# A tower of patch embedding, 16-head attention and a quantised layer: two pieces of the embedding weights loaded ahead of the second patch tile

## The chip, the core and the metric

The kernel runs on one core of a Trainium2 chip. The core has a matrix engine (TensorE, PE in the profile, with PEld for its weight loads), three engines for elementwise work (VectorE or DVE, ScalarE or ACT, GpSimd or POOL) and a sync engine (SP), which here issues all the transfers between the chip's main memory (HBM) and the on-chip memory. Each engine works through its own list of instructions in order; engines wait for one another by semaphores. The metric is the device time of one execution in microseconds (us).

## What is computed

```python
# tok: x (64, 125, 64) -> 448 rows of 1024 (64 batches x 7 patches)
x = x[:, :n_patch * TIN, :].reshape(bsz, n_patch, TIN * F)
x = layer_norm(x, g1, b1, 1e-6)
x = jnp.einsum('bpd,dh->bph', x, W) + b          # 1024 -> 512
h = layer_norm(x, g2, b2, 1e-6)
# attention: 16 heads of 128, causal, inside each batch of 7 rows
h = h + attn(layernorm(h, 1e-5))
# a linear layer on values rounded to fp8 with one scale for all
h = h + ffn(layernorm(h, 1e-5))
```

All of it is in fp32; products in attention and in the last layer are made of three fp32r products of high and low parts.

## The kernel before

The 448 rows are cut into four tiles of 112 rows (`TILES`, `TR`). The input width of 1024 is cut into eight chunks of 128 (`KIN`). For each tile t the embedding has these steps:

- `patch_moments(t)` on DVE (line 777 for the statistics, 779 for their aggregate) waits for the tile's patches; `rsqrt` turns the variance into a reciprocal root. For the tiles named in `ROOTS` ScalarE takes a square root first (`take_root`, line 569) and DVE mends it in three short steps (`rsqrt_from_root`, lines 795 to 805); for the others DVE works out the root alone in eight steps (lines 821 to 829). Line 837 makes the shift `nmr`.
- `normalise(t)` on ACT (line 574) applies scale and shift.
- `patch_transposes(t)` on PE (line 309) turns the eight chunks, `patch_evacuate(t)` on ACT (line 583) brings them back as `xt`, scaled by g1 and shifted by b1.
- `embed(t, half)` on PE (line 320) multiplies four chunks by `tokw_raw`, the weights of 1024 x 512, which come in four pieces of two chunks (`TOKW_PIECES`). After the second half a short product adds the bias (line 325). For tile 0 it waits for `tok_b_lo_ok`.
- `stream_norms` on DVE then normalises the embedded tile from `acc[t]`; `normalise_stream` (ACT, line 592), `stream_transposes` (PE, line 336), `stream_evacuate` (ACT) and `stream_lo` (DVE, line 770) give `ht_hi` and `ht_lo`, from which the attention's products of line 280 to 282 read. Three tiles must be there before the first of them.

The order is written out by hand in each engine's list. Three places of it matter here. SP issues its transfers in the order of lines 238 to 260, all in one queue, with no wait before the one of `ffn_b_cleared`. PE's list is the loop behind `patch_transposes(0)`: half of a tile's product, the next tile's transposes, the other half. And the bias is split into high and low part on two engines: ACT makes the high part at line 614 (shown as L563, the helper), behind `normalise(1)`; DVE makes the low part in `bias_lo` (shown as L770), which is placed inside the root of tile 2, behind its sixth step:

```python
need(rsqrt([(2, LN_EPS)], patch_moments(2), between=lambda i: bias_lo() if i == 5 else None))
```

So `bias_lo` comes behind `patch_moments(2)`, which waits for the patches of tile 2. Behind it DVE waits for `rows_landed` (g2 and b2, the last two transfers of this stage) before tile 3.

Of the kernel before, what the change touches and what calls it, by code (L numbers as in the profile page):

```python
# [21 lines left out]
TILES = 4  # L22
TR = ROWS // TILES
KIN = IN_DIM // 128
# [11 lines left out]
LN_EPS, NORM_EPS = 1e-6, 1e-5  # L36


ROOTS = {0: LN_EPS, 2 * TILES + 1: NORM_EPS, TILES + 2: LN_EPS, 2 * TILES + 2: NORM_EPS,
         TILES + 3: LN_EPS, 2 * TILES + 3: NORM_EPS}  # L40
FP8_MAX, SCALE_EPS = 448.0, 1e-7
SHIFT_20 = 2.0 ** 20
# [8 lines left out]
def audio_tower(nc, patches, tok_w, heads_w, ffn_w, tok_g1, tok_b1, tok_b, tok_g2, tok_b2,  # L51
# [4 lines left out]
    with ExitStack() as ctx:  # L56
        def sb(name, shape, dt=F32):
            return ctx.enter_context(nc.sbuf_tensor(name, shape, dt))

        def sem(name):  # L60
            return ctx.enter_context(nc.semaphore(name))
# [14 lines left out]
        x_in = sb("x_in", [TR, TILES, IN_DIM])  # L76
# [48 lines left out]
        nmr = sb("nmr", [TR, NCOL])  # L125
        eps_4 = sb("eps_4", [TR, len(ROOTS)])
        root = sb("root", [TR, len(ROOTS)])
        last_root = sb("last_root", [TR, TILES])
# [20 lines left out]
        x_landed = [sem(f"x_landed{t}") for t in range(TILES)]  # L149
# [72 lines left out]
        def loop_heads(eng, step):  # L222

            with eng.Fori(0, (HEADS - 2) // 2) as i:
                step(i * 2 + 1, i, 1)
                step(i * 2 + 2, i + 1, 0)


        @block.sync
        def _(sp):  # L230
            def load(dst, src, landed):
                sp.dma_start(dst, src).then_inc(landed, 16)  # L232

            def load_tokw(i):
                a, b = TOKW_PIECES[i]
                load(tokw_raw[:, a:b, :], tok_w[:, a:b, :], tokw_landed[i])

            for c, landed in ((slice(0, 512), x_landed[0]), (slice(512, IN_DIM), x0_rest_landed)):
                load(x_in[:, 0, c], patches[0][:, c], landed)
            load(ident_sb[:], ident, ident_landed)  # L240
            load(g1_col[:], tok_g1, cols_landed)
            load(b1_col[:], tok_b1, cols_landed)
            load(x_in[:, 1, :], patches[1], x_landed[1])
            load_tokw(0)
            load_tokw(1)
            load_tokw(2)
            load(x_in[:, 2, :], patches[2], x_landed[2])
            load_tokw(3)
            load(tok_b_raw[:], tok_b, tok_b_landed)
            load(x_in[:, 3, :], patches[3], x_landed[3])  # L250
            load(g2_row[:], tok_g2.to_broadcast([TR, D]), rows_landed)
            load(b2_row[:], tok_b2.to_broadcast([TR, D]), rows_landed)
            load(mask_sb[:], mask, late_landed)
            load(ffn_scale_col[:], ffn_scale.to_broadcast([128, 1]), late_landed)
            sp.wait_ge(ffn_b_cleared, 1)
            for row in (0, B_LO):
                load(ffn_b_raw[row:row + 1, :], ffn_bias, late_landed)
            for s in range(2):
                sp.dma_start(raw[:, s, :], heads_w[s]).then_inc(raw_landed[s], 16)
            sp.dma_start(ffnw_raw[:], ffn_w).then_inc(ffnw_landed, 16)  # L260

            def load_head(h, _, s):


                sp.wait_ge(outw_hi_ok, h)
                sp.wait_ge(outw_lo_ok, h)
                sp.dma_start(raw[:, 1 - s, :], heads_w[h + 1]).then_inc(raw_landed[1 - s], 16)

            loop_heads(sp, load_head)
            for i, (t, c) in enumerate(RESULTS):  # L270
                sp.wait_ge(y_ok, i + 1)
                sp.dma_start(out[t][:, c], h_sb[:, t, c]).then_inc(out_stored, 16)
            sp.wait_ge(out_stored, 16 * len(RESULTS))
# [3 lines left out]
        def _(pe):  # L277
# [19 lines left out]
            def patch_transposes(t):  # L297
                if t == 0:
                    pe.wait_ge(ident_landed, 16)
                    pe.wait_ge(x0_half_normed, 1)  # L300
                else:
                    pe.wait_ge(x_normed, t + 1)
                if t >= 2:
                    pe.wait_ge(xt_ok, KIN * (t - 1))
                for k in range(KIN):
                    if t == 0 and k == KIN // 2:
                        pe.wait_ge(x_normed, 1)
                    b = 2 * (t % 2) + k // 4
                    mm = nc.tensor.transpose(bank[b][:, k % 4 * TR:(k % 4 + 1) * TR],
                                             x_in[:, t, k * 128:(k + 1) * 128], ident_sb[0:TR, 0:TR])  # L310
                    if k % 4 == 3:
                        mm.then_inc(xt_ps, 1)

            def embed(t, half):
                for k in range(half * KIN // 2, (half + 1) * KIN // 2):
                    for i, (first_chunk, _) in enumerate(TOKW_PIECES):
                        if t == 0 and k == first_chunk:
                            pe.wait_ge(tokw_landed[i], 16)
                    pe.wait_ge(xt_ok, KIN * t + k + 1)
                    nc.tensor.matmul(acc[t][0:TR, :], xt[:, t % 2, k * TR:(k + 1) * TR], tokw_raw[:, k, :],  # L320
                                     start=(k == 0), stop=False, skip_group_check=True)
                if half == 1:
                    if t == 0:
                        pe.wait_ge(tok_b_lo_ok, 1)
                    nc.tensor.matmul(acc[t][0:TR, :], ones_r[:], tok_b_split[:], start=False, stop=True,
                                     skip_group_check=True).then_inc(tok_ps, 1)


            def stream_transposes(t):
                pe.wait_ge(hn_ok, t + 1)  # L330
                if t <= 1:
                    pe.wait_ge(xt_ok, KIN * (TILES - 1))
                if t == 2:
                    pe.wait_ge(xt_ok, KIN * TILES)
                for k in range(KD):
                    last = nc.tensor.transpose(ht_bank[t][:, k * TR:(k + 1) * TR],
                                               hn_sb[:, t, k * 128:(k + 1) * 128], ident_sb[0:TR, 0:TR])
                last.then_inc(ht_ps, 1)
# [14 lines left out]
            patch_transposes(0)  # L353
            for t in range(TILES):
                embed(t, 0)
                if t + 1 < TILES:
                    patch_transposes(t + 1)
                else:
                    stream_transposes(1)
                embed(t, 1)  # L360
                if t == TILES - 2:
                    stream_transposes(0)
# [198 lines left out]
        def _(act):  # L561
# [3 lines left out]
            def take_root(c):  # L565
                i = list(ROOTS).index(c)
                act.wait_ge(variance_ok, i + 1)
                act.wait_ge(eps_ok, len(ROOTS))
                nc.scalar.activation(root[:, i:i + 1], moments[:, c, 1:2], ACT.Sqrt, bias=eps_4[:, i:i + 1],
                                     scale=4.0).then_inc(root_ok, 1)  # L570

            def normalise(t, c=slice(0, IN_DIM)):
                act.wait_ge(x_scaled, t + 1)
                nc.scalar.activation(x_in[:, t, c], x_in[:, t, c], ACT.Identity, bias=nmr[:, t:t + 1],
                                     scale=rstd[:, t:t + 1]).then_inc(x_normed, 1)

            def patch_evacuate(t):
                for half in range(2):
                    act.wait_ge(xt_ps, 2 * t + half + 1)
                    if t >= 2 and half == 0:  # L580
                        act.wait_ge(tok_ps, t - 1)
                    for k in range(half * KIN // 2, (half + 1) * KIN // 2):
                        nc.scalar.activation(xt[:, t % 2, k * TR:(k + 1) * TR],  # L583
                                             bank[2 * (t % 2) + half][:, k % 4 * TR:(k % 4 + 1) * TR],
                                             ACT.Identity, bias=b1_col[:, k:k + 1],
                                             scale=g1_col[:, k:k + 1]).then_inc(xt_ok, 1)
# [22 lines left out]
            normalise(0, slice(IN_DIM // 2, IN_DIM))  # L609
            act.wait_ge(cols_landed, 32)  # L610
            patch_evacuate(0)
            normalise(1)
            act.wait_ge(tok_b_landed, 16)
            hi_part(tok_b_split[:], tok_b_raw[:]).then_inc(tok_b_hi_ok, 1)
# [138 lines left out]
        def _(dve):  # L753
# [18 lines left out]
            def moments_of(c, parts, rest_landed=None):  # L772
# [6 lines left out]
                aggregate = nc.vector.bn_aggr(moments[:, c, :], stats[:, c, 0:len(parts), :])  # L779
                if c not in ROOTS:  # L780
                    return mark(aggregate)
                aggregate.then_inc(variance_ok, 1)

            def need_moments(c, step):
                if c in ROOTS:
                    dve.wait_ge(variance_ok, list(ROOTS).index(c) + 1)
# [340 lines left out]
```

## Time and profile before

| | |
|---|---|
| median of 3 runs | 275.11 us (274.51 to 275.82) |
| the profiled execution | 274.97 us, span 273.2 us |
| PE busy | 263.6 us of the span |
| DVE busy, ACT busy | 156.8 us, 129.9 us |
| read from HBM | 22.56 MB |

In the profile L12 is line 12 of the kernel; times within the span are in us from its start. The last 1.8 us of the execution's own time lie outside the span. The attention heads fill the span from about 57 to 246 us with PE busy throughout; the stage that the change touches is the first 57 us. A row of a timeline gives start, duration, engine, line, operation, output and input, the count of instructions, and in brackets how long the engine stood idle before it and what released it. A matmul in fp32 stands in the profile as two instructions, so four chunks of line 320 are a row of x8.

### The profile page before, as it was taken

How to read it: one execution, taken by the hardware profiler on the slowest of the kernel's cores; microseconds unless marked ns; L12 is line 12 of the kernel's file. 1: busy time of each engine (PE TensorE's matmuls, PEld its weight loads, DVE VectorE, ACT ScalarE, POOL GpSimd, SP SyncE). 2: the span in 40 equal slices, each digit the busy share in tenths (PEclk: the TensorE clock that was granted, in tenths of full speed). 3: DMA queues.
4: the chain of work that ended last, by engine and by line, in shares of the span. 5: the costliest groups of instructions: out<-in, count | busy, mean ns of one | idle time of the engine just before them, and what ended most of it. 6: DMA issues, size and time to landing. Idle time of an engine off the chain costs nothing.

```text
span 273.2 us, 3833 instructions
## 1 busy us (share of the span) xinstructions
PE 263.6 (97%) x1444; PEld 220.4 (81%) x1444; DVE 156.8 (57%) x322; ACT 129.9 (48%) x221; POOL 0.2 (0%) x4
## 2 busy tenths in 40 slices
PE   7799998999999999999999999999999999999895
PEld 7434446999999999999999999999999999985363
DVE  6479969655555446263555455362645453579782
ACT  2663952454435444544535344435444354365460
POOL 0000000000000000000000000000000000000000
PEclk9999999999999999999999999999999999999799
DMA  6998000134214040403123040404132100000004
GB/s 191 309 289 366 2 0 1 29 127 154 82 74 151 2 154 0 154 6 148 52 102 116 37 154 0 154 0 154 17 137 86 67 0 0 0 4 0 0 0 134
DMA packets 5319, 23.57 MB, mean 86 GB/s; under 512 B 1005, under 2 KB 1469, under 8 KB 3136
## 3 DMA queue, kind: packets, MB, share of 16 engines
q1 hardware_dynamic: 5312, 23.48, 25.3%
q8 instruction: 4, 0.07, 0.1%
q14 instruction: 3, 0.02, 0.0%
HBM read 22.56 MB, written 0.92 MB: 86 GB/s over the span
## 4 chain that ended last, share of the span: by engine, by line
PE 75%; DVE 9%; ACT 5%; DMA 4%; SPq 3%; issue 2%; DVEq 0%; ACTq 0%
PE bank L280 15%; PE bank L281 15%; PE bank L282 15%; PE acc L422 8%; PE bank L406 5%; PE bank L398 5%; PE acc L426 4%; DMA b_row<-tok_b 4%; SPq L232 3%; PE bank L412 2%; PE bank L391 2%; PE acc L541 2%; ACT xt L583 2%; DVE stats L777 1%; DVE ffnw_lo L770 1%
## 5 line engine op out<-in xcount | busy, mean ns | idle before, releaser
L280 PE MATMUL bank<-ht_hi,qkvw_hi 128*128 128x448 f32 (+2 forms) x204 | 74.7, 366 | 0.1
L281 PE MATMUL bank<-ht_lo,qkvw_hi 128*128 128x448 f32 (+2 forms) x204 | 73.3, 359 | 0.0
L282 PE MATMUL bank<-ht_hi,qkvw_lo 128*128 128x448 f32 (+2 forms) x204 | 73.2, 359 | 0.0
L770 DVE TENSOR_TENSOR qkvw_lo<-raw,qkvw_hi 128x1536 fp32r<-128x1536 f32 x16 | 28.1, 1758 | 30.8 <-ACT qkvw_hi L563 30.8
L280 PEld LDWEIGHTS bank<-ht_hi,qkvw_hi 128*128 128x128 f32 x204 | 38.4, 188 | 3.3 <-issue 0.3
L282 PEld LDWEIGHTS bank<-ht_hi,qkvw_lo 128*128 128x128 f32 x204 | 38.3, 188 | 3.3
L281 PEld LDWEIGHTS bank<-ht_lo,qkvw_hi 128*128 128x128 f32 x204 | 38.4, 188 | 3.0
L770 DVE TENSOR_TENSOR z_lo<-bank,z_hi 128x448 fp32r<-128x448 f32 x15 | 9.4, 624 | 43.2 <-ACT z_hi L563 43.2
L320 PE MATMUL acc<-tokw_raw,xt 128*112 128x512 f32 x64 | 29.3, 598 | 1.5 <-DMA tokw_raw<-tok_w 1.5
L563 ACT CAST qkvw_hi<-raw 128x1536 fp32r<-128x1536 f32 x16 | 23.6, 1482 | 0.0
L320 PEld LDWEIGHTS acc<-tokw_raw,xt 128*112 128x112 f32 x64 | 10.6, 177 | 14.7 <-issue 9.6
L659 ACT COPY v_t<-bank 128x448 f32<-128x448 f32 x16 | 8.5, 532 | 28.4 <-PE bank L282 28.4
L422 PE MATMUL acc<-z_hi,outw_hi 128*128 128x448 f32 x56 | 21.7, 388 | 0.0
L651 ACT COPY q_t<-bank 128x448 f32<-128x448 f32 x16 | 8.5, 531 | 26.3 <-PE bank L282 26.3
L422 PE MATMUL acc<-z_hi,outw_lo 128*128 128x448 f32 x56 | 20.6, 368 | 0.0
L642 ACT ACTIVATE prob<-prob 112x448 f32<-112x448 f32 x16 | 9.3, 578 | 18.6 <-DVE prob L946 18.6
L398 PEld LDWEIGHTS bank<-prob_t,v_nat 112*128 112x128 f32 x128 | 16.7, 191 | 0.7
L398 PE MATMUL bank<-prob_t,v_nat 112*128 112x112 f32 x128 | 16.7, 273 | 0.0
L950 DVE TENSOR_REDUCE ssum<-prob 112x4 f32<-112x448 f32 x16 | 9.9, 619 | 9.9 <-ACT prob L642 9.9
L406 PE MATMUL bank<-k_t,q_t 128*112 128x112 f32 x128 | 15.2, 262 | 0.0
L663 ACT COPY v_nat<-bank 112x512 f32<-112x512 f32 x16 | 9.4, 587 | 10.4 <-PE bank L412 10.4
L406 PEld LDWEIGHTS bank<-k_t,q_t 128*112 128x112 f32 x128 | 13.9, 178 | 0.1
(128 smaller groups left out, 350.4 us busy)
## 6 DMA issues: line engine op xcount, KB each, us to landing
raw<-heads_w SPq DMA_DIRECT2D x16, 1024.0 KB, 4.8
tokw_raw<-tok_w SPq DMA_DIRECT2D x4, 512.0 KB, 7.1
x_in<-patches SPq DMA_DIRECT2D x3, 448.0 KB, 9.1
ffnw_raw<-ffn_w SPq DMA_DIRECT2D x1, 1024.0 KB, 16.8
out<-h_sb SPq DMA_DIRECT2D x3, 224.0 KB, 2.3
x_in<-patches SPq DMA_DIRECT2D x2, 224.0 KB, 2.9
g_row<-tok_g SPq DMA_DIRECT2D x1, 224.0 KB, 10.6
b_row<-tok_b SPq DMA_DIRECT2D x1, 224.0 KB, 11.1
```

The lines of the kernel that those rows point to most:

```text
L280: nc.tensor.matmul(ps, hi, whi, start=first, stop=False, skip_group_check=True)
L281: nc.tensor.matmul(ps, hi, wlo, start=False, stop=False, skip_group_check=True)
L282: return nc.tensor.matmul(ps, lo, whi, start=False, stop=last, skip_group_check=True)
L320: nc.tensor.matmul(acc[t][0:TR, :], xt[:, t % 2, k * TR:(k + 1) * TR], tokw_raw[:, k, :], start=(k == 0), stop=False, skip_group_check=True)
L398: last = nc.tensor.matmul(bank[b][:, t * TR:(t + 1) * TR], v_nat[:, t, :], prob_t[:, t, :], start=True, stop=True)
L406: last = nc.tensor.matmul(bank[1][0:TR, c], q_t[:, c], k_t[:, c], start=True, stop=True)
L422: nc.tensor.matmul(acc[c][:, 0:ROWS], w[:, c * 128:(c + 1) * 128], all_rows(z_hi), start=False, stop=False, skip_group_check=True)
L426: last = nc.tensor.matmul(acc[c][:, 0:ROWS], outw_hi[s][:, c * 128:(c + 1) * 128], all_rows(z_lo), start=False, stop=False, skip_group_che ...
L563: return nc.scalar.copy(dst, src)
L663: nc.scalar.copy(v_nat[:].rearrange("p t e -> p (t e)"), bank[3][0:TR, :]).then_inc(vn_ok, 1)
L770: return nc.vector.tensor_tensor(dst, src, hi.bitcast(F32), ALU.subtract)
L950: nc.vector.tensor_reduce(ssum[:], prob[:], AX.X, ALU.add).then_inc(softmax_step, 1)
```

## The change

The transfers of the first two weight pieces go ahead of tile 1's patches, and tile 2's patches go behind all four weight pieces and the bias. Tile 1 joins `ROOTS`, so ScalarE takes its square root ahead of `normalise(1)`. On PE tile 0's product is no longer cut in the middle: tile 1's transposes stand behind its seventh chunk, and the loop goes on to tile 1 with `continue`. Nothing else is moved; `bias_lo` keeps its place. Adding an entry to `ROOTS` also adds one short memset on DVE. In the later lines the numbers grow by 2 to 6.

```diff
-ROOTS = {0: LN_EPS, 2 * TILES + 1: NORM_EPS, TILES + 2: LN_EPS, 2 * TILES + 2: NORM_EPS,
+ROOTS = {0: LN_EPS, 1: LN_EPS, 2 * TILES + 1: NORM_EPS, TILES + 2: LN_EPS, 2 * TILES + 2: NORM_EPS,
...
-            load(x_in[:, 1, :], patches[1], x_landed[1])
             load_tokw(0)
             load_tokw(1)
+            load(x_in[:, 1, :], patches[1], x_landed[1])
             load_tokw(2)
-            load(x_in[:, 2, :], patches[2], x_landed[2])
             load_tokw(3)
             load(tok_b_raw[:], tok_b, tok_b_landed)
+            load(x_in[:, 2, :], patches[2], x_landed[2])
             load(x_in[:, 3, :], patches[3], x_landed[3])
...
-            def embed(t, half):
+            def embed(t, half, within=None):
...
+                    if k == KIN - 2 and within is not None:
+                        within()
...
                 embed(t, 0)
+                if t == 0:
+                    embed(t, 1, within=lambda: patch_transposes(1))
+                    continue
                 if t + 1 < TILES:
                     patch_transposes(t + 1)
...
             patch_evacuate(0)
+            take_root(1)
             normalise(1)
```

The first place is SP's queue at the start of the program. Patches are `x_in`, weight pieces `tokw_raw` (x2 are two of them). Before:

```order
L232 DMA b_col<-tok_b 128x8
L232 DMA x_in<-patches 112x1024
L232 DMA tokw_raw<-tok_w 128x1024 x3
L232 DMA x_in<-patches 112x1024
L232 DMA tokw_raw<-tok_w 128x1024
L232 DMA tok_b_raw<-tok_b 33x512
L232 DMA x_in<-patches 112x1024
L232 DMA g_row<-tok_g 112x512
```

And now:

```order
L232 DMA b_col<-tok_b 128x8
L232 DMA tokw_raw<-tok_w 128x1024 x2
L232 DMA x_in<-patches 112x1024
L232 DMA tokw_raw<-tok_w 128x1024 x2
L232 DMA tok_b_raw<-tok_b 33x512
L232 DMA x_in<-patches 112x1024 x2
L232 DMA g_row<-tok_g 112x512
```

Tile 2's patches moved past the last weight piece and the bias; what is issued up to and with the bias before is the same set of transfers that is now issued up to and with tile 2's patches.

The second place is PE from the first chunk of tile 0 to the first chunks of tile 1. Before:

```order
L320 MATMUL acc<-tokw_raw,xt 112x512 [waits xt_ok,tokw_landed0]
L320 MATMUL acc<-tokw_raw,xt 112x512 [waits xt_ok]
L320 MATMUL acc<-tokw_raw,xt 112x512 [waits xt_ok,tokw_landed1]
L320 MATMUL acc<-tokw_raw,xt 112x512 [waits xt_ok]
L309 MATMUL bank<-ident_sb,x_in 128x112 [waits x_normed]
L309 MATMUL bank<-ident_sb,x_in 128x112 x7
L320 MATMUL acc<-tokw_raw,xt 112x512 [waits xt_ok,tokw_landed2]
L320 MATMUL acc<-tokw_raw,xt 112x512 [waits xt_ok]
L320 MATMUL acc<-tokw_raw,xt 112x512 [waits xt_ok,tokw_landed3]
L320 MATMUL acc<-tokw_raw,xt 112x512 [waits xt_ok]
L325 MATMUL acc<-tok_b_split,ones_r 112x512 [waits tok_b_lo_ok]
L320 MATMUL acc<-tokw_raw,xt 112x512 [waits xt_ok] x4
```

And now:

```order
L320 MATMUL acc<-tokw_raw,xt 112x512 [waits xt_ok,tokw_landed2]
L320 MATMUL acc<-tokw_raw,xt 112x512 [waits xt_ok]
L320 MATMUL acc<-tokw_raw,xt 112x512 [waits xt_ok,tokw_landed3]
L309 MATMUL bank<-ident_sb,x_in 128x112 [waits x_normed]
L309 MATMUL bank<-ident_sb,x_in 128x112 x7
L320 MATMUL acc<-tokw_raw,xt 112x512 [waits xt_ok]
L327 MATMUL acc<-tok_b_split,ones_r 112x512 [waits tok_b_lo_ok]
L320 MATMUL acc<-tokw_raw,xt 112x512 [waits xt_ok] x4
```

The transposes of tile 1 (line 309) moved from behind the fourth chunk to behind the seventh; the bias product with its wait still stands ahead of all of tile 1's product.

The third place is DVE, from the end of tile 1's root to the low part of the bias. Before:

```order
L829 SCALAR_TENSOR_TENSOR rstd<-newton,rstd 112x1 [waits dve_step]
L837 SCALAR_TENSOR_TENSOR nmr<-moments,rstd 112x1 [waits dve_step]
L777 BN_STATS stats<-x_in 112x6 [waits x_landed2]
L777 BN_STATS stats<-x_in 112x6
L779 BN_AGGR moments<-stats 112x2 [waits dve_step]
L821 TENSOR_SCALAR vscaled<-moments 112x1 [waits dve_step]
L824 TENSOR_SCALAR rstd<-vscaled 112x1 [waits dve_step]
L827 TENSOR_SCALAR newton<-rstd,vscaled 112x1 [waits dve_step]
L829 SCALAR_TENSOR_TENSOR rstd<-newton,rstd 112x1 [waits dve_step]
L827 TENSOR_SCALAR newton<-rstd,vscaled 112x1 [waits dve_step]
L829 SCALAR_TENSOR_TENSOR rstd<-newton,rstd 112x1 [waits dve_step]
L770 TENSOR_TENSOR tok_b_split<-tok_b_raw,tok_b_split 1x512 [waits tok_b_hi_ok]
```

And now:

```order
L811 SCALAR_TENSOR_TENSOR rstd<-newton,rstd 112x1 [waits dve_step]
L843 SCALAR_TENSOR_TENSOR nmr<-moments,rstd 112x1 [waits dve_step]
L783 BN_STATS stats<-x_in 112x6 [waits x_landed2]
L783 BN_STATS stats<-x_in 112x6
L785 BN_AGGR moments<-stats 112x2 [waits dve_step]
L827 TENSOR_SCALAR vscaled<-moments 112x1 [waits dve_step]
L830 TENSOR_SCALAR rstd<-vscaled 112x1 [waits dve_step]
L833 TENSOR_SCALAR newton<-rstd,vscaled 112x1 [waits dve_step]
L835 SCALAR_TENSOR_TENSOR rstd<-newton,rstd 112x1 [waits dve_step]
L833 TENSOR_SCALAR newton<-rstd,vscaled 112x1 [waits dve_step]
L835 SCALAR_TENSOR_TENSOR rstd<-newton,rstd 112x1 [waits dve_step]
L776 TENSOR_TENSOR tok_b_split<-tok_b_raw,tok_b_split 1x512 [waits tok_b_hi_ok]
```

Tile 1's root now ends with line 811, behind ACT's square root. From the wait for tile 2's patches (`x_landed2`) on, DVE's list is as it was: the low part of the bias (L770, now L776) stands nine instructions behind that wait.

## Rows read from the trace of the kernel before

**Rows 1.** The chain in order of time, 0 to 45 us: start, us, what.

```profile
8.34 11.10 DMA b_row<-tok_b
```

**Rows 2.** Timeline of PE, 8.9 to 45.6 us.

```profile
9.17 3.69 PE L320 MATMUL acc<-tokw_raw,xt 128*112 128x512 f32 x8 [1.23 <-DMA tokw_raw<-tok_w]
12.70 0.93 PE L309 MATMUL bank<-ident_sb,x_in 112*128 112x112 f32 x8
13.47 1.88 PE L320 MATMUL acc<-tokw_raw,xt 128*112 128x512 f32 x4
15.60 1.97 PE L320 MATMUL acc<-tokw_raw,xt 128*112 128x512 f32 x4 [0.24 <-DMA tokw_raw<-tok_w]
17.74 0.48 PE L325 MATMUL acc<-tok_b_split,ones_r 33*112 33x512 f32 x1 [0.17 <-DVE tok_b_split L770]
18.15 3.69 PE L320 MATMUL acc<-tokw_raw,xt 128*112 128x512 f32 x8
...
42.49 0.49 PE L325 MATMUL acc<-tok_b_split,ones_r 33*112 33x512 f32 x1
43.59 0.60 PE L336 MATMUL bank<-ident_sb,hn_sb 112*128 112x112 f32 x4 [0.61 <-ACT hn_sb L592]
...
45.57 0.39 PE L280 MATMUL bank<-ht_hi,qkvw_hi 128*128 128x336 f32 x1
```

**Rows 3.** Timeline of SP, its transfers as they are issued.

```profile
3.54 1.38 SPq L232 DMA_DIRECT2D tokw_raw<-tok_w  x3
4.96 0.56 SPq L232 DMA_DIRECT2D x_in<-patches  x1
5.56 0.85 SPq L232 DMA_DIRECT2D tokw_raw<-tok_w  x1
```

**Rows 4.** From issue to landing: second and third weight piece, tile 2's patches, last piece.

```profile
DMA to landing us min/median/max: 6.4/7.1/7.8
...
DMA to landing us min/median/max: 9.1/9.1/9.1
...
DMA to landing us min/median/max: 10.0/10.0/10.0
```

**Rows 5.** Timeline of ACT, 0 to 17 us.

```profile
6.42 0.82 ACT L574 ACTIVATE x_in<-x_in,nmr,rstd 112x512 f32<-112x512 f32 x1 [0.93 <-DVE nmr L837]
7.66 2.79 ACT L583 ACTIVATE xt<-bank,b_col,g_col 128x112 f32<-128x112 f32 x8 [0.43 <-PE bank L309]
10.75 1.24 ACT L574 ACTIVATE x_in<-x_in,nmr,rstd 112x1024 f32<-112x1024 f32 x1 [0.30 <-DVE nmr L837]
15.97 0.62 ACT L563 CAST tok_b_split<-tok_b_raw 33x512 fp32r<-33x512 f32 x1 [3.98 <-DMA tok_b_raw<-tok_b]
```

**Rows 6.** Timeline of DVE, 0 to 45 us.

```profile
4.95 0.21 DVE L779 BATCH_NORM_AGGREGATE moments<-stats 112x2 f32<-112x12 f32 x1
...
8.42 0.21 DVE L779 BATCH_NORM_AGGREGATE moments<-stats 112x2 f32<-112x12 f32 x1
...
14.06 1.28 DVE L777 BATCH_NORM_STATS2 stats<-x_in 112x6 f32<-112x512 f32 x2 [3.35 <-DMA x_in<-patches]
...
17.00 0.68 DVE L770 TENSOR_TENSOR tok_b_split<-tok_b_raw,tok_b_split 1x512 fp32r<-1x512 f32 x1
...
18.22 0.16 DVE L837 SCALAR_TENSOR_TENSOR nmr<-moments,rstd 112x1 f32<-112x1 f32 x1
19.47 1.28 DVE L777 BATCH_NORM_STATS2 stats<-x_in 112x6 f32<-112x512 f32 x2 [1.09 <-DMA b_row<-tok_b]
...
43.14 0.69 DVE L777 BATCH_NORM_STATS2 stats<-acc 112x6 f32<-112x512 f32 x1
```

**Rows 7.** Busy time and granted clock (PEclk) by stretch, near the span's end.

```profile
255.00:256.00 1.00, 0.29 (x1) 0.29 (x2) 0.56 (x5) 0.00 (x0) 0.00 (x0) 0.66 0.00 0
256.00:257.00 1.00, 1.00 (x5) 0.52 (x5) 0.47 (x3) 0.00 (x0) 0.00 (x0) 0.50 0.00 0
...
258.00:259.00 1.00, 1.00 (x4) 0.30 (x2) 0.87 (x3) 1.00 (x3) 0.00 (x0) 0.64 0.00 0
```

**Rows 8.** The same view where PE waits for the first weight piece.

```profile
8.00:9.00 1.00, 0.00 (x0) 0.00 (x0) 0.90 (x4) 1.00 (x5) 0.00 (x0) 1.00 0.83 324
```

## The prediction

> **What bounds the kernel now.** I read the chain of waits in order of time first. It starts in the transfers: its longest link is the landing of b2, issued at 8.34 and landed 11.10 us later, at 19.44 [rows 1]. From there it runs over DVE and ACT until PE takes over at about 43.6. The change works earlier than that, so I read PE's timeline next. PE waits 1.23 us for the first weight piece (starts at 9.17), 0.24 us for the fourth (15.60) and 0.17 us for the low part of the bias (17.74); from 18.15, where tile 1's product starts, to 42.98 (42.49 + 0.49) no row of it shows a wait [rows 2]. So in this stage two chains run almost side by side: DVE and ACT from b2's landing, and PE from 18.15 with nothing but its own work. Their distance is small. PE waits 0.61 us for ACT at 43.59, but DVE begins the statistics of the last tile at 43.14, only 0.16 us after PE's last product ends [rows 2, 6], and behind those statistics in DVE's list stands the low part of tile 2's `ht`, which the first attention products wait for (45.57). A PE chain that ends over 0.1 us later (taking some 0.05 us of the 0.16 for the signal) therefore moves the start of the attention by the same amount. From there PE is busy through the heads, so a delay of that start is a delay of the end.
>
> **Part 1: the order of the transfers.** They are issued from one queue within a few us, long before they land, so it is their order that counts, not the issue (about 0.45 us each). Landings before: second weight piece 4.0 + 6.4 = 10.4 (the three are issued from 3.54 on), third 4.5 + 7.8 = 12.3, tile 2's patches 4.96 + 9.1 = 14.06, fourth piece 5.56 + 10.0 = 15.56 [rows 3, 4], the bias just before ACT's cast of it at 15.97 [rows 5]. If the queue is drained in its order, a transfer lands when the bytes ahead of it and its own are through, whatever their order. This gives the new landings without any bandwidth:
> - tile 1's patches have now ahead of them what the second weight piece had: 10.4.
> - the third piece: 12.3, as before.
> - tile 2's patches have ahead what the bias had: **15.9 instead of 14.06, so 1.84 us later**. Bounds: not before 15.6, since the fourth piece needs until 15.56 and patches are behind it; not much after 16.3, since the row lengths and byte counts are the same.
> - the fourth piece is ahead of 448 KB that took 14.06 - 12.3 = 1.76 us: 15.56 - 1.76 = 13.8, or 14.2 if these bytes move slower, as the 1.84 above suggests. I take 14.2. The bias: about 14.3.
> - g2 and b2 see the same bytes ahead: 19.44 as before.
>
> The Trainium skill, page "DMA: Bandwidth & Descriptors", section "Queues, rings and completion order", says that each engine takes its share in ring order, but that completions are not first in, first out per issuer. By that a set of transfers may close slightly out of order; here the landings before all follow the order of issue [rows 3 to 5], and it is the reason for my third rival.
>
> **Part 2: what PE gains.** The first weight piece now lands at about 7.5 (no row; it lies between its issue and 9.14). ACT's evacuation, one chunk each 0.35 us from 7.66 [rows 5], has the first chunk ready at about 8.1, so PE starts 1.05 us earlier. The next chunks take 0.9 us each (3.6 us for four) [rows 2]: two until 9.9, two more (their piece has landed by about 9.3, an estimate between 7.5 and the 10.4 of what follows it) until 11.7; then PE waits for the third piece (12.3), does two until 14.1, the seventh from 14.2 to 15.1, tile 1's transposes 0.77 us (13.47 - 12.70), the eighth until 16.8. Before, the eighth ended at 17.57 (15.60 + 1.97). PE has gained 0.8 us and stands before the bias product.
>
> **Part 3: what it waits for there.** The bias product waits for its low part, which DVE makes inside the root of tile 2. DVE began tile 2's statistics as the patches landed, at 14.06, and the low part at 17.00, 2.94 us behind, by nothing but its own instructions; PE had it at 17.74, 3.68 us behind [rows 2, 6]. That part of DVE's list is unchanged. With patches at 15.9 the statistics start at 15.9, the low part at 18.84, and PE's bias product at 15.9 + 3.68 = **19.58**, where it was 17.74. All of tile 1's product stands behind it on PE: 19.99 in place of 18.15. So PE is idle from 16.8 to 19.6, 2.8 us, and the 0.8 us of part 2 are swallowed there. The high part is no limit: the bias lands at 14.3, ACT is free of tile 1's normalisation at 14.5 (below), cast 0.62 us, 15.1.
>
> **Part 4: ScalarE's root.** Tile 0, with the root on ACT, needed 6.42 - 4.95 = 1.47 us from the aggregate to the normalisation; tile 1, on DVE alone, 10.75 - 8.42 = 2.33 us [rows 5, 6]. It saves 0.86 us. Tile 1's patches land at 10.4 now, statistics 1.29 us, aggregate at 11.75, normalised from 13.2 to 14.5. Its reader, PE's transposes, comes at 15.1, and even 0.86 us later it would cost under 0.3 us ahead of an idle 2.8 us. Worth: nothing on the path. ACT waits in front of its root, but has nothing to do there. The extra memset (0.1 us) ends before the first patches land. Tile 1's evacuation starts at about 15.5 and ends at 18.4, ahead of PE's use at 20.
>
> **Part 5: DVE and ACT behind it.** DVE is through with tile 2 at 18.22 + 1.84 = 20.06, where b2's landing let it start tile 3 at 19.47 [rows 6]. So DVE's and ACT's chain moves by 0.65 us. It stays inside PE's delay: PE's chain is 1.84 us late, and DVE meets it again at tile 1's statistics. ACT keeps pace and becomes no bound.
>
> **Sum with the full clock.** +1.84 at the start of tile 1's product; no wait in the 24.8 us of PE work behind it that could give anything back [rows 2]; -0.1 us slack at tile 3's statistics: **+1.75 us**. On the profiled execution (span 273.2, whole 274.97, which is 0.14 under the median) that is 276.7; on the median of 275.11 it is 276.9.
>
> **Part 6: TensorE's clock.** The new wait of 2.8 us is longer than any in the rows. Near the end the granted clock fell from full (2.4 GHz) to 0.50 (1.2 GHz) at about 255.3, after 4 us of separate short products and an idle 0.85 us, and rose again at about 258.7: 0.68 us of the stretch 255 to 256 at the lower level, all of the next (one row shown), 0.72 us of 258 to 259, 3.4 us in all [rows 7]. At the first weight piece PE idled 1.23 us in front of busy transposes and the clock stayed at 1.00 [rows 8]. The new gap is more than twice as long as either, with half a us of idle before it (11.7 to 12.3) and one short burst between. If the clock falls as at 255, some 3.4 us pass at half rate; as far as they lie on PE's back-to-back products they cost half, 1.7 us; if the fall comes up to 1 us before the gap ends, 1.2 us. I take 1.45. From 0 (the row of 1.23 us) to 1.7: nearest to the new case is the fall, since the gap is the longer one, so I forecast it: 276.85 + 1.45 = **278.3**.
>
> The Trainium skill, page "TensorE: Matmul & The Clock Gate", section "Part 1: The HAM clock gate", says that the slow rate is the default and activity releases it. The trace agrees, with 0.50 granted behind the thin stretch at 255; no row before says what a gap of 2.8 us does in front of a busy stretch.
>
> **Rivals.**
> - *The clock stays at full rate* (for: no fall at 1.23 us idle; against: the fall at 255 after less idleness). Time 276.5 to 277.3, likeliest 276.9.
> - *Only part of the delay arrives*: patches of tile 2 land at 15 rather than 15.9, or DVE's statistics of the last tile have more slack than 0.1. Each us of earlier landing is worth one us: 275.3 to 276.4.
> - *Faster: landing does not follow the order of the queue.* Place: tile 2's patches. If they land by 14.1 in spite of their place, the low part of the bias comes at 17.0 and PE starts tile 1 at 18.15 or sooner; the decisive point is a landing at 14.0. Then DVE's chain from b2 still holds the end, so the gain is what b2 lands earlier, 0 to 1.2 us: 273.9 to 275.1. Against it: all landings before are in order.
> - *A worse one*: the clock falls for longer, or the last patches and b2 also land later, since DVE reads them; 279 to 280.5.
>
> **Chances.** Clock falls: 0.46 (277.8 to 278.8). Clock stays: 0.34. Part of the delay: 0.09. Landing out of order: 0.06. Worse: 0.05. The range leaves out the worst, the faster one and most of the part: 276.1 to 279.0. A measurement of this kernel can tell about 0.5% (1.4 us) from no change. Slower by more than that is above 276.5: both first cases and the worst, less a little of the second: 0.83. Within 0.5%: 0.13. Faster: 0.04.
>
> **What would show it.** In the profile of the changed kernel: tile 2's patches issued behind the bias and DVE's statistics of them at 15.6 to 16.3, released by their landing; the low part of the bias at about 18.8; PE idle 2.4 to 3 us in front of the bias product at about 19.6, released by DVE; tile 1's product from 20.0; the first product of line 280 at 47.3 with the full clock, at 48.8 with the lower one, and then a granted clock of 0.50 for some us between 17 and 24. The first chunk at about 8.1 and the root of tile 1 from ACT at 12 show parts 2 and 4. The forecast is wrong if the patches land near 14, or if PE's wait at the bias is under 1 us.

## The result, and the profile after

The change makes the kernel slower: a median of 278.26 us over 20 runs, against 274.78 us for the kernel before on 20 runs beside it, a ratio of 1.0128 with a 95% interval of 1.0112 to 1.0145. The ratios here and below leave out the few executions in a slower state of the chip and are not quotients of the medians given, from which they differ by up to 0.3%. The runs of the change lie widely apart, from 275.89 to 280.23 us; the experiments explain a part of that. The profiled execution took 279.33 us with a span of 277.5, 4.3 us over the 273.2 of the kernel before.

The chain is the path of waits that ended last, followed back from the last instruction. The first row below gives each engine's share of it, PE 84%; the next rows are the chain in order of time, between 0 and 52 us (start, us, what). Where the chain of before went through b2's landing [rows 1], it now goes through the landing of the patches that moved back.

```profile
PE 84%; DVE 7%; DMA 3%; SPq 2%; ACT 2%; issue 1%; DVEq 0%; ACTq 0%
```

```profile
6.43 9.27 DMA x_in<-patches
20.17 6.51 PE acc L320 x8
27.45 3.44 PE acc L320 x8
```

PE's timeline from 6.5 us on (start, duration, engine, line, operation, operands, count, idle time before and its releaser) answers to [rows 2]:

```profile
8.20 3.66 PE L320 MATMUL acc<-tokw_raw,xt 128*112 128x512 f32 x8 [0.30 <-ACT xt L588]
12.14 2.90 PE L320 MATMUL acc<-tokw_raw,xt 128*112 128x512 f32 x6 [0.28 <-DMA tokw_raw<-tok_w]
15.02 0.99 PE L309 MATMUL bank<-ident_sb,x_in 112*128 112x112 f32 x8
15.85 1.02 PE L320 MATMUL acc<-tokw_raw,xt 128*112 128x512 f32 x2
19.40 0.77 PE L327 MATMUL acc<-tok_b_split,ones_r 33*112 33x512 f32 x1 [2.53 <-DVE tok_b_split L776]
20.10 6.58 PE L320 MATMUL acc<-tokw_raw,xt 128*112 128x512 f32 x8
...
50.21 0.39 PE L280 MATMUL bank<-ht_hi,qkvw_hi 128*128 128x336 f32 x1 [0.69 <-DVE ht_lo L776]
```

PE starts 0.97 us earlier than before (8.20 against 9.17) and is through with tile 0's chunks at 16.87 (15.85 + 1.02). Then it stands idle for 2.53 us, released by the low part of the bias. The bias product comes 1.66 us later than before (19.40 against 17.74). And tile 1's first half takes 6.58 us where it took 3.69, the bias product 0.77 where it took 0.48: together 3.18 us more for the same work. The first attention product starts at 50.21 instead of 45.57, 4.64 us later; the rest of the span is 227.3 us against 227.6, so 0.3 us came back later. In this execution the clock does not fall near the end as it did in [rows 7].

DVE's timeline shows who holds up the bias. It answers to [rows 6]:

```profile
15.72 1.29 DVE L783 BATCH_NORM_STATS2 stats<-x_in 112x6 f32<-112x512 f32 x2 [2.03 <-DMA x_in<-patches]
...
18.67 0.68 DVE L776 TENSOR_TENSOR tok_b_split<-tok_b_raw,tok_b_split 1x512 fp32r<-1x512 f32 x1
...
31.34 0.70 DVE L783 BATCH_NORM_STATS2 stats<-acc 112x6 f32<-112x512 f32 x1 [4.42 <-PE acc L327]
...
47.77 0.70 DVE L783 BATCH_NORM_STATS2 stats<-acc 112x6 f32<-112x512 f32 x1 [1.10 <-PE acc L327]
```

Tile 2's patches are there at 15.7 instead of 14.06, and the low part follows 2.95 us behind them (before: 2.94). Later DVE waits 4.42 and 1.10 us for PE: the chain of DVE and ACT has become the one with room.

The stretches of the same trace (length, busy time of PE, PEld, DVE, ACT and POOL with counts, granted clock, DMA share, GB/s) show the rest:

```profile
18.00:19.00 1.00, 0.00 (x0) 0.00 (x0) 0.90 (x4) 0.46 (x2) 0.00 (x0) 1.00 1.27 295
19.00:20.00 1.00, 0.60 (x1) 0.26 (x1) 0.90 (x5) 0.00 (x0) 0.00 (x0) 0.57 0.97 346
20.00:21.00 1.00, 1.00 (x2) 0.45 (x2) 1.00 (x3) 0.92 (x1) 0.00 (x0) 0.50 0.99 410
...
24.00:25.00 1.00, 1.00 (x2) 0.31 (x1) 1.00 (x8) 0.00 (x0) 0.00 (x0) 0.50 1.04 418
25.00:26.00 1.00, 1.00 (x2) 0.31 (x1) 0.93 (x3) 0.66 (x1) 0.00 (x0) 0.52 0.96 401
26.00:27.00 1.00, 1.00 (x8) 0.62 (x6) 0.88 (x2) 0.58 (x1) 0.00 (x0) 1.00 0.49 188
```

The granted clock falls to 0.50 (1.2 GHz) at about 19.1 (0.57 on average over that us), while PE is idle, and is back at full rate only at about 26.0: some 6.8 us, where the fall near the end of the kernel before lasted 3.4 [rows 7].

### The profile page after: what moved, and what is told of

Read it like the earlier page. It is cut to its first block, busy times and chain, and to the rows that moved or that the text cites. A ratio compares the mean times of both kernels' runs of the same rounds, so it can differ in the third digit from the quotient of the medians.

```text
span 277.5 us, 3833 instructions
## 1 busy us (share of the span) xinstructions
PE 265.1 (96%) x1444; PEld 220.4 (79%) x1444; DVE 156.0 (56%) x319; ACT 130.5 (47%) x222; POOL 0.2 (0%) x4
## 4 chain that ended last, share of the span: by engine, by line
PE 84%; DVE 7%; DMA 3%; SPq 2%; ACT 2%; issue 1%; DVEq 0%; ACTq 0%
PE bank L280 15%; PE bank L281 15%; PE bank L282 15%; PE acc L320 9%; PE acc L427 8%; PE bank L411 5%; PE bank L403 4%; PE acc L431 4%; DMA x_in<-patches 3%; PE bank L417 2%; PE bank L396 2%; PE acc L546 2%; SPq L232 2%; DVE ffnw_lo L776 1%; ACT hn_sb L718 1%
## 5 line engine op out<-in xcount | busy, mean ns | idle before, releaser
L776 DVE TENSOR_TENSOR qkvw_lo<-raw,qkvw_hi 128x1536 fp32r<-128x1536 f32 x16 | 28.1, 1758 | 30.7 <-ACT qkvw_hi L568 30.7
L776 DVE TENSOR_TENSOR z_lo<-bank,z_hi 128x448 fp32r<-128x448 f32 x15 | 9.4, 624 | 43.2 <-ACT z_hi L568 43.2
L320 PE MATMUL acc<-tokw_raw,xt 128*112 128x512 f32 x64 | 32.2, 648 | 0.6 <-ACT xt L588 0.3
L320 PEld LDWEIGHTS acc<-tokw_raw,xt 128*112 128x112 f32 x64 | 11.5, 192 | 15.8 <-issue 12.3
L669 ACT COPY v_nat<-bank 112x512 f32<-112x512 f32 x16 | 9.4, 586 | 10.4 <-PE bank L417 10.4
```

Of the source, the lines that this page charges most:

```text
L669: nc.scalar.copy(v_nat[:].rearrange("p t e -> p (t e)"), bank[3][0:TR, :]).then_inc(vn_ok, 1)
L776: return nc.vector.tensor_tensor(dst, src, hi.bitcast(F32), ALU.subtract)
```

## The experiments

The theory of the prediction: tile 2's late patches hold up the low part of the bias, that holds up all of PE's list behind it, and the idle time lowers the clock. The rivals: the transfers' new order costs by itself, through the late patches and with no part of the bias; the transposes' new place or the root on ScalarE costs; or the clock has no part. Medians of before differ a little from chip to chip, so each ratio is against the runs of before on its own chip: 275.38 us for the first four kernels, 274.50 us for the others.

### The low part of the bias ahead of the patches

```diff
+            bias_lo()
-            need(rsqrt([(2, LN_EPS)], patch_moments(2), between=lambda i: bias_lo() if i == 5 else None))
+            need(rsqrt([(2, LN_EPS)], patch_moments(2)))
```

> The changed kernel, with the low part of the bias taken out of tile 2's root and placed on DVE ahead of the wait for tile 2's patches. Theory (the late patches hold up the low part, it holds up PE, and PE's idleness lowers the clock): the low part is ready at about 16.2, PE's bias product at about 17.0, tile 1's product from 17.4, no fall of the clock in the first 30 us, and all of the loss is gone: 274.5 to 275.3 us. Rival (the new order of transfers costs by itself, since tile 2's patches and with them DVE's and ACT's chain are 1.7 us late): 276 us or more. Rival (the transposes behind the seventh chunk cost): 275.5 to 276.5.

Measured: 275.1 us, ratio 0.9996 (0.9971 to 1.0021), so no loss that can be measured is left once one instruction is moved. PE's timeline of this kernel:

```profile
15.78 1.02 PE L320 MATMUL acc<-tokw_raw,xt 128*112 128x512 f32 x2
16.73 0.48 PE L327 MATMUL acc<-tok_b_split,ones_r 33*112 33x512 f32 x1
17.14 3.69 PE L320 MATMUL acc<-tokw_raw,xt 128*112 128x512 f32 x8
21.10 0.99 PE L309 MATMUL bank<-ident_sb,x_in 112*128 112x112 f32 x8 [0.27 <-ACT x_in L579]
...
26.69 3.69 PE L320 MATMUL acc<-tokw_raw,xt 128*112 128x512 f32 x8 [0.76 <-ACT xt L588]
...
43.83 0.60 PE L338 MATMUL bank<-ident_sb,hn_sb 112*128 112x112 f32 x4 [0.63 <-ACT hn_sb L597]
...
45.80 0.39 PE L280 MATMUL bank<-ht_hi,qkvw_hi 128*128 128x336 f32 x1
```

PE has no wait at the bias, the first half of tile 1's product takes 3.69 us again, and it starts 1.0 us ahead of the kernel before. Yet the first attention product starts at 45.80, 0.2 us behind the 45.57 of before. PE gives the 1.0 us back where it waits 0.27 and 0.76 us for ACT, at the normalisation and the evacuation of tile 2: tile 2's patches land as late as in the change (issued at 6.3, landed 9.2 us later), and the early weights and the late patches cancel out. Near the end of the stage PE waits 0.63 us for ACT, as before (0.61). So beside the bias the late patches cost no more than this head start and 0.2 us, and the transposes' new place and the root, which are in this kernel too, leave nothing that can be measured. None of the three carries the loss of the change.

### The transfers alone

```diff
 # the kernel before, with this order only
-            load(x_in[:, 1, :], patches[1], x_landed[1])
             load_tokw(0)
             load_tokw(1)
+            load(x_in[:, 1, :], patches[1], x_landed[1])
             load_tokw(2)
-            load(x_in[:, 2, :], patches[2], x_landed[2])
             load_tokw(3)
             load(tok_b_raw[:], tok_b, tok_b_landed)
+            load(x_in[:, 2, :], patches[2], x_landed[2])
```

> The kernel before with nothing but the new order of transfers; root and transposes as before. Theory: PE stands at tile 1's transposes behind the fourth chunk, from about 11.8 to 15.9 (patches at 10.9, root on DVE alone, normalised at 15.8), then does four chunks and reaches the bias product at about 20.3, later than the low part at 19.4; tile 1's product from 20.7, 2.6 us later than before, and an idle 4 us that lowers the clock: 278 to 281 us. Rival (the loss comes from the position of the transposes, not from the transfers): 275 us.

Measured: 279.94 us over 6 executions, ratio 1.0162 (1.0114 to 1.0211). PE's timeline, then the granted clock by stretches:

```profile
15.90 1.76 PE L309 MATMUL bank<-ident_sb,x_in 112*128 112x112 f32 x8 [3.66 <-ACT x_in L574]
17.45 5.51 PE L320 MATMUL acc<-tokw_raw,xt 128*112 128x512 f32 x8
22.89 0.48 PE L325 MATMUL acc<-tok_b_split,ones_r 33*112 33x512 f32 x1
```

```profile
15.00:17.00 2.00, 1.10 (x6) 1.10 (x7) 0.96 (x2) 1.41 (x3) 0.00 (x0) 0.50 1.02 262
17.00:19.00 2.00, 2.00 (x6) 1.07 (x5) 1.72 (x9) 2.00 (x7) 0.00 (x0) 0.50 1.18 298
19.00:21.00 2.00, 2.00 (x4) 0.76 (x3) 1.90 (x6) 1.35 (x4) 0.00 (x0) 0.50 0.96 378
```

The wait is where it was expected, in front of tile 1's transposes, since with the old order of PE the late patches of tile 1 are asked for behind the fourth chunk. It is 3.66 us long, the clock falls here too, and the low rate makes 5.51 us of a half of a product that takes 3.60 at full rate (the second half of tile 1's, at 27.59 of this trace). PE reaches the bias at 22.89, 2.6 us later than expected, for the clock was not in that part of the expectation. So with PE's old order the new transfers cost by another path, tile 1's patches, with no wait for the low part of the bias. Whether the other two edits soften the loss is not shown: the intervals of the two ratios overlap, and the first attention product starts at 50.53 here and at 50.21 in the change.

### The order of PE and the root, without the transfers

```diff
 # the changed kernel, with the old order of the transfers
```

> The changed kernel with the old order of transfers, so only the root on ScalarE and the transposes behind the seventh chunk. Theory: tile 2's patches land at 14.1 and the low part of the bias is there at 17.7 as before; PE waits for the fourth weight piece at 15.6, does the seventh chunk, transposes, the eighth, and reaches the bias at about 18.2, 0.5 us later than before; over 0.1 of it arrives: 275.0 to 275.6 us, clock at full rate. Rival (root or transposes carry the loss of the change): 277 us or more.

Measured: 275.26 us, ratio 0.9999 (0.9971 to 1.0028). The bias product starts at 18.07, 0.33 us later than before, the first attention product at 45.70, 0.13 later, and the clock does not fall in the profiled execution. Transposes and root carry no loss that can be measured.

### The gap filled

```diff
                     if t == 0:
+                        keep_warm(13, bank[0])
                         pe.wait_ge(tok_b_lo_ok, 1)
```

> The changed kernel with 13 warming products of 112 columns (some 2.4 us, result unused) on PE in the gap in front of the bias product; nothing else is touched, so the low part of the bias is as late as in the change. Theory: the delay of 1.9 us stays (tile 1's product from about 20.1), the granted clock stays at full rate, and 276.5 to 277.0 us are left of the 278.3: the clock's share is 1.3 to 1.8 us. Rival (the clock has no part, the whole loss is the wait): 278.3 us as in the change. Rival (the fall has another cause than idleness): granted clock of 0.50 behind 19 us all the same.

Measured: 276.54 us, ratio 1.0071 (1.0039 to 1.0104). PE's timeline and the clock:

```profile
16.82 2.72 PE L288 MATMUL bank<-ones_sb 112*112 112x112 f32 x26
19.47 0.48 PE L328 MATMUL acc<-tok_b_split,ones_r 33*112 33x512 f32 x1
19.88 3.69 PE L320 MATMUL acc<-tokw_raw,xt 128*112 128x512 f32 x8
...
47.11 0.39 PE L280 MATMUL bank<-ht_hi,qkvw_hi 128*128 128x336 f32 x1 [0.69 <-DVE ht_lo L777]
```

```profile
17.00:19.00 2.00, 2.00 (x23) 2.00 (x22) 1.72 (x9) 1.57 (x5) 0.00 (x0) 1.00 1.15 298
19.00:21.00 2.00, 2.00 (x10) 1.15 (x9) 1.90 (x6) 0.93 (x1) 0.00 (x0) 1.00 0.98 401
```

The bias product is as late as in the change, 19.47, and with PE kept busy by work whose result nobody reads the clock stays at full rate through this stage (it falls once, for 3.4 us, near the end of the kernel, as before). The start of the attention is 1.54 us late instead of 4.64.

One profile would not show that the fill did this, since the change itself keeps the clock in some executions (below). But the mean granted clock of each whole execution is on record. With 3.4 us at half rate it comes to about 0.994, with 6.8 us to 0.988. In the change it is 0.986 to 0.988 in 12 of the 20 executions and 0.992 to 0.994 in the other 8; with the gap filled it is 0.998 or more in 9 of 12 and never under 0.992. So the fill does keep the clock up, and the rival without the clock falls, as does the one that saw another cause in its fall.

In ratios, 0.71% is left of 1.28%: the clock's share of the loss is 0.57%, 1.6 us. By the medians it is 2.3 us, since 1.16 us are left of 3.48, and the two intervals together allow anything from about 0.6 to 2.6 us (an estimate that takes them as independent). One thing stays open: with the gap filled, four executions with a mean clock of 1.00 took 277.26 to 278.96 us, where four others with 1.00 took 276.04 to 276.50. Something other than the clock adds up to 2.9 us in some executions, and no trace taken shows what.

### Tile 2's patches ahead of the fourth weight piece

```diff
             load_tokw(2)
+            load(x_in[:, 2, :], patches[2], x_landed[2])
             load_tokw(3)
             load(tok_b_raw[:], tok_b, tok_b_landed)
-            load(x_in[:, 2, :], patches[2], x_landed[2])
```

> The changed kernel with one transfer put back: tile 2's patches ahead of the fourth weight piece, so the first two weight pieces are still early; DVE's list is that of the change. Theory (tile 2's patches set the low part of the bias): patches land at about 14.1, low part at 17.0, PE waits for the fourth piece at 15.6 and reaches the bias at about 18.2, tile 1's product from 18.5, clock at full rate: 275.0 to 275.6 us. Rival (tile 1's later patches, behind two weight pieces, are the cause): still 277 us or more.

Measured: 275.56 us, ratio 1.0032 (1.0014 to 1.0051). One transfer put back takes three quarters of the loss away (0.32% left of 1.28%), with tile 1's patches still behind two weight pieces. DVE's timeline, then PE's:

```profile
14.06 1.29 DVE L783 BATCH_NORM_STATS2 stats<-x_in 112x6 f32<-112x512 f32 x2 [0.61 <-DMA x_in<-patches]
...
17.01 0.68 DVE L776 TENSOR_TENSOR tok_b_split<-tok_b_raw,tok_b_split 1x512 fp32r<-1x512 f32 x1
```

```profile
15.66 1.11 PE L320 MATMUL acc<-tokw_raw,xt 128*112 128x512 f32 x2 [1.37 <-DMA tokw_raw<-tok_w]
...
18.33 0.48 PE L327 MATMUL acc<-tok_b_split,ones_r 33*112 33x512 f32 x1
```

The patches and the low part are at the times of before to 0.01 us. What remains is that the transposes now stand behind the seventh chunk, which waits for the fourth weight piece: the bias product is 0.59 us late and the first attention product 0.40 (45.97). The early start of PE has all gone into the 1.37 us of waiting for that piece. The 0.32% that are left are 0.9 us (0.4 to 1.4), so a part of them may be something else.

### The wait for g2 and b2 moved back, in the kernel before

```diff
+            moments_3 = patch_moments(3)
             dve.wait_ge(rows_landed, 32)
-            stream_norms(0, None, patch=(3, patch_moments(3)))
+            stream_norms(0, None, patch=(3, moments_3))
```

> The kernel before, with DVE's wait for g2 and b2 moved from ahead of tile 3's patch statistics to behind them. Theory (two chains side by side, PE's from 18.15 with no wait in it): DVE starts tile 3 at about 18.2 instead of 19.5, DVE and ACT run over 1 us ahead, and PE's chain holds the start of the attention: gain 0 to 0.2 us, 274.6 to 275.0 us. Rival (the chain of waits from the landing of b2 is what bounds): 1.2 us faster.

Measured: 274.52 us, ratio 1.0 (0.9979 to 1.002). DVE does start tile 3 at 18.10 instead of 19.47 and then waits for PE at the last tile:

```profile
18.10 1.28 DVE L777 BATCH_NORM_STATS2 stats<-x_in 112x6 f32<-112x512 f32 x2
...
42.94 0.70 DVE L777 BATCH_NORM_STATS2 stats<-acc 112x6 f32<-112x512 f32 x1 [1.05 <-PE acc L325]
```

The link that took most of the chain before, 11.10 us [rows 1], is worth 0.2 us when 1.4 of it are taken away (first attention product at 45.38 against 45.57). This is the other half of the picture of two chains side by side: the early PE of the first experiment met DVE and ACT, the early DVE of this one meets PE.

### Both chains shortened

```diff
-ROOTS = {0: LN_EPS, 1: LN_EPS,
+ROOTS = {0: LN_EPS, 1: LN_EPS, 2: LN_EPS,
...
-            patch_evacuate(1)
+            patch_evacuate(1, amid=lambda: take_root(2))
```

with `bias_lo` ahead of the patches and the wait for g2 and b2 moved back, as above. `amid` is called between the two halves.

> The changed kernel with the low part of the bias ahead of the wait for tile 2's patches, tile 2's root on ScalarE too (between the two halves of tile 1's evacuation), and the wait for g2 and b2 behind tile 3's patch statistics. Theory: PE starts tile 1's product at 17.2 as in the experiment with the bias first, 1 us ahead of the kernel before, and now DVE is done with tile 2 at about 18.9 and tile 3's and tile 0's statistics come 0.5 us earlier than before; the start of the attention moves from 45.6 to about 45.1: 274.3 to 274.8 us. Rival (something else holds the stage): 275.1 us, as with the bias first alone.

Measured: 274.27 us, ratio 1.0002 (0.998 to 1.0024): no difference from the kernel before that can be measured. Its transfers landed some 0.3 us later than in the other profiles (tile 1's statistics at 11.25 against 10.94), PE started tile 1's product at 17.53, and DVE tile 3's statistics at 19.21, 0.3 us ahead of before instead of the expected 0.5. The first attention product started at 45.33, 0.24 us earlier. The expected 0.5 us is not there, and no version found here beats the kernel before beyond what can be measured.

### The change once more

> The changed kernel once more, for one look at another execution. The wait in front of the bias product is 2.5 us again, and tile 1's product starts at 20.1; the granted clock falls to 0.50 somewhere between 17 and 22 us for one or two stretches of 3.4 us, or stays at 1.00, and the time goes with it: 276.0 with no fall, 277.7 with one, 279.3 with two on full work.

Measured: 275.97 us, a single execution. Its timeline of PE and its clock:

```profile
19.21 0.49 PE L327 MATMUL acc<-tok_b_split,ones_r 33*112 33x512 f32 x1 [2.45 <-DVE tok_b_split L776]
19.62 3.69 PE L320 MATMUL acc<-tokw_raw,xt 128*112 128x512 f32 x8
...
46.84 0.39 PE L280 MATMUL bank<-ht_hi,qkvw_hi 128*128 128x336 f32 x1 [0.69 <-DVE ht_lo L776]
```

```profile
19.00:20.00 1.00, 0.79 (x2) 0.44 (x3) 0.90 (x5) 0.12 (x1) 0.00 (x0) 1.00 0.94 352
20.00:21.00 1.00, 1.00 (x3) 0.35 (x2) 1.00 (x2) 1.00 (x1) 0.00 (x0) 1.00 0.99 410
```

The same program, nearly the same wait (2.45 us against 2.53), and no fall in this stage; near the end the clock falls for 3.4 us. It took 3.36 us less than the profiled execution above, and the first attention product started 3.37 us earlier, so the two executions differ in that stretch alone: 0.19 us by the landing, 3.18 us by the clock. A gap of 2.5 us is thus one at which the clock falls in some executions and not in others.

This explains a part of how far the change's runs lie apart, and not all. A mean clock of 0.992 to 0.994 is some 3.3 to 4.4 us at half rate, which can cost at most half of that, and still seven of the executions that show it spread from 275.89 to 279.17 us. The rest has the open cause met with the gap filled.

## Why the prediction was right, point by point

The forecast was 278.3 us, the measured median is 278.26, and the range of 276.1 to 279.0 holds it. That the two agree so closely is partly luck: two terms were off and cancelled.

- **Landings by sets of transfers.** Tile 2's patches: 15.9 forecast, 15.72 measured (15.53 in the second profile of the change). Tile 1's patches: 10.4 forecast, 10.94 measured. In the profile of the change the transfers of this stage land in the order of issue, and in no run did the rival with landings out of order show.
- **The low part and PE's wait.** Forecast 18.84 and an idle 2.8 us; measured 18.67 and 2.53 us. The distance from patches to low part was 2.95 us, as read (2.94). The early start of PE was forecast at 8.1 and came at 8.20.
- **The delay at the attention.** Forecast 1.75 us, of a shift of 1.84 less 0.1 of slack. Without the clock it measured 1.27 us (second profile: bias 1.47 late) and 1.54 us (gap filled: bias 1.73 late). The landing was earlier than taken, and the slack is 0.2, not 0.1: the 24.8 us of PE work "with no wait in it" held a stop of 0.08 us before, at tile 2's product (26.46, where the bias product of tile 1 starts at 25.97 and takes 0.41), which came back. This term was 0.2 to 0.5 us too large. The sum with the full clock, 276.9, stands against 275.97 in the second profile and a median of 276.54 with the gap filled.
- **The clock.** The step "some 3.4 us pass at half rate", priced at 1.2 to 1.7 us, was read from the one fall of the trace before [rows 7] and failed: in the profiled execution the low rate lasted 6.8 us, with PE busy from 19.40 on, and cost 3.18 us. In the other direction, it does not fall in every execution. The median loss of 3.48 us less the 1.3 to 1.5 of delay leaves about 2 us for the clock and for the open cause of the spread together, against 1.45 forecast for the clock; by the gap filled the clock's part is 1.6 us in ratios and 2.3 in medians. The step took one execution's price as the typical one, where it is a mixture from 0 to over 3 us. The prediction also reads [rows 8] as an idle 1.23 us "in front of busy transposes"; what follows that wait are the products of line 320, at 9.17 [rows 2]. That the clock held there stays true.
- **The rule of the clock page.** The Trainium skill, page "TensorE: Matmul & The Clock Gate", section "Part 1: The HAM clock gate", says the slow rate is the default and activity releases it. The filled gap bears this out: 26 short matmul instructions in place of 2.5 us of idleness, and the granted clock is 1.00 from 17 to 21 us. The same section calls the number of slow matmuls at a kernel's start run-variable. No run here measures that start, but the fall in mid-kernel varied too: idle for 2.53 us with a fall, for 2.45 us with none.
- **The root on ScalarE and the memset.** Worth nothing on the path, as forecast: tile 1 was normalised from 13.73 to 14.97, and PE's transposes of it started at 15.02, behind the seventh chunk. 0.86 us later they would still have been ahead of an idle 2.53 us; this is an argument, for no run leaves out the root alone. With the transfers alone the same 0.9 us lies inside PE's 3.66 us of waiting, and there it should have counted.
- **DVE and ACT stay inside.** Tile 3's statistics began at 19.96, 0.49 us later than before (0.65 forecast), and DVE waited 4.42 us for PE at tile 1 and 1.10 at tile 3. In the experiment with the bias first DVE reaches the last step of tile 2 at 19.61 (18.22 before) and PE is not late; there the lateness takes PE's head start of 1.0 us and 0.2 us more.

## What to carry to other kernels

When a transfer is moved back in a queue, follow not only its reader but everything that stands behind the reader's wait in that engine's list: here a 0.68 us helper for another tile, placed there to fill a bubble, became the release of the busiest engine. A piece loaded earlier makes another one land later: here, even with the helper moved out of the way, the early weights won nothing, because PE met the late patches one tile further on. And if such a wait leaves TensorE idle for some us in front of dense work, count the clock as a term of its own, as a mixture over executions and not as one number.

## What the runs showed of the hardware

- A fall of the granted clock can outlast the idleness by far: idle until 19.40, full rate again at 26.0, with matmuls back to back between. With the transfers alone PE was back at 15.90 and the clock at about 21.3. In the kernel before the fall near the end lasted 3.4 us.
- The same program with the same idle time (2.45 and 2.53 us) kept the clock once and lost it once; the executions differed by 3.36 us. With short useless matmuls in the gap the profiled execution kept it, and the mean granted clock was 0.998 or more in 9 of 12 executions, against none of 20 without them.
- With one queue and transfers of 448 and 512 KB, landings followed the order of issue in the profiles of before and of the change, and a permuted set closed within 0.6 us of where the same set had closed before (10.94 against 10.4, 15.72 against 15.9).
- Executions of one program with the same mean clock of 1.00 differed by 2.9 us (276.04 and 278.96, gap filled); the cause is not known.
